# Expert results in four tables ordered by when a token's experts run; three tables are loaded and added while the last three experts run

## The reference, cut to what matters

```python
w, idx = _gate(xf, wg)                      # 4 of 32 experts for each token, with weights
fe = idx.reshape(-1)
pos = (cumsum(one_hot(fe)) * one_hot(fe)).sum(-1) - 1
dest = where(pos < cap, fe * cap + pos, E * cap)      # cap = 640 rows for each expert
xe = xp[buf_tok].reshape(E, cap, DIM)
h = silu(xe @ w1) * (xe @ w3)               # for each expert
out = (h @ w2) * buf_w
y = zeros.at[buf_tok].add(out)              # a token gets the sum of its four results
z = silu(xf @ sw1) * (xf @ sw3) @ sw2       # the shared expert
x = layernorm(xf + y + z)
```

## Time and profile before

| | us |
|---|---|
| median of three runs | 968.32 (965.99 to 975.98) |
| profiled execution | 962.11 |
| its span, first to last instruction | 960.4 |

### The profile page before, as it was taken

One profiled execution on the slowest core, in us unless ns is written; L12 is line 12 of the kernel. 1 busy time (PEld: TensorE's weight loads), 2 busy tenths in 40 slices (PEclk: granted clock), 3 DMA queues, 4 the chain that ended last, 5 costly groups with the idle time before them and its releaser, 6 DMA issues.

```text
span 960.4 us, 26130 instructions
## 1 busy us (share of the span) xinstructions
PE 817.0 (85%) x9489; PEld 594.5 (62%) x9489; DVE 673.9 (70%) x2532; ACT 650.1 (68%) x1262; POOL 681.7 (71%) x580
## 2 busy tenths in 40 slices
PE   4889999999999999999999999873377778786765
PEld 2367777777777777777777777762145555554532
DVE  6667788987987987987897897766255445545417
ACT  3678888888888798898798787864155444444405
POOL 7556565699699689689779869654656576676646
PEclk9799999999999999999999999997789898989979
DMA  5697797743453355345434433133358676566448
GB/s 159 152 297 220 241 249 202 188 121 97 97 147 98 71 140 131 73 108 133 104 90 125 116 80 98 35 91 93 74 117 175 150 168 139 144 152 140 103 157 302
DMA packets 164432, 133.88 MB, mean 139 GB/s; under 512 B 69907, under 2 KB 131654, under 8 KB 163408
## 3 DMA queue, kind: packets, MB, share of 16 engines
q1 hardware_dynamic: 155408, 116.60, 47.4%
q0 software_dynamic: 8896, 15.61, 5.7%
HBM read 31.19 MB, written 39.49 MB: 74 GB/s over the span
## 4 chain that ended last, share of the span: by engine, by line
PE 63%; issue 9%; DVE 7%; DMA 6%; ACT 6%; SPq 5%; another core or an unknown queue 3%; POOL 1%; ACTq 0%; DVEq 0%; POOLq 0%
PE PS L1328 8%; PE PS L1385 6%; PE PS L1359 4%; PE PS L1409 4%; PE PS L1392 4%; PE PS L1390 4%; PE PS L1342 3%; PE PS L1224 3%; PE PS L1411 3%; PE PS L1410 3%; PE PS L1438 3%; PE PS L1439 3%; PE PS L1183 3%; SPq L2503 2%
## 5 line engine op out<-in xcount | busy, mean ns | idle before, releaser
L2328 POOL TENSOR_TENSOR PL<-PF,PH 128x1280 f16<-128x1280 f32 x121 | 317.7, 2626 | 105.6 <-ACT PH L1674 66.6
L1943 DVE CUSTOM_DVE_ANT_0 JUNK<-PS,M 128x256 f16<-128x256 f32 (+3 forms) x512 | 225.3, 485 | 43.6 <-PE PS L1359 40.8
L1668 ACT ACTIVATE PF<-PS 128x512 f32<-128x512 f32 (+1 forms) x384 | 193.2, 520 | 77.3 <-PE PS L1392 74.3
L2371 POOL DMA_INDIRECT y_rows<-BIG,PLACE x150 | 153.0, 1020 | 85.7 <-ACT BIG L1568 48.0
L1674 ACT ACTIVATE PH<-PF 128x1280 f16<-128x1280 f32 x128 | 162.2, 1267 | 0.6
L2361 POOL DMA_INDIRECT xe_rows<-PAY,DEST x128 | 130.2, 1017 | 43.8 <-issue 27.7
L1385 PE MATMUL PS<-Q,K 128*128 128x512 f16 (+3 forms) x512 | 147.9, 299 | 6.9 <-DMA Q<-MROW 3.7
L1409 PE MATMUL PS<-VH,PH 128*128 128x65 f16 x1280 | 140.2, 195 | 11.4 <-DVE Y L1985 7.4
L1411 PE MATMUL PS<-VH,PL 128*128 128x65 f16 x1280 | 140.1, 193 | 0.1
L1410 PE MATMUL PS<-VL,PH 128*128 128x64 f16 x1280 | 140.1, 194 | 0.0
L1409 PEld LDWEIGHTS PS<-VH,PH 128*128 128x128 f16 x1280 | 119.1, 97 | 31.2 <-issue 20.1
(11 more groups left out here) (287 smaller groups left out, 2146.6 us busy)
## 6 DMA issues: line engine op xcount, KB each, us to landing
K<-KH SPq DMA_DIRECT2D x128, 128.0 KB, 2.3
Q<-QH SPq DMA_DIRECT2D x128, 128.0 KB, 2.4
xe_rows<-PAY SPq DMA_DIRECT2D x20, 520.0 KB, 4.1
Q<-xe_rows SPq DMA_DIRECT2D x30, 325.0 KB
K<-KL SPq DMA_DIRECT2D x64, 128.0 KB, 2.3
Q<-QL SPq DMA_DIRECT2D x64, 128.0 KB, 2.4
y_rows<-PAY SPq DMA_DIRECT2D x16, 512.0 KB, 4.9
K<-in_L_ffn_w_dram SPq DMA_DIRECT2D x78, 64.0 KB
```

The source lines that it names most:

```text
L1668: e.activation(PF[:, n % PBUF, c0:c0 + width], PS[:, k, 0:width], ACT.Exp).then_inc(s["c_exp"], 1)
L1943: e.tensor_tensor_reduce(JUNK[:, n_ttr % 2, 0:width], PS[:, base + ab, c0:c0 + width], M0[:, 512 - width:512], 1.0, -3e38, ALU.add, ALU.ma ...
L2328: e.tensor_tensor(PL[:, n % PBUF, :], PF[:, n % PBUF, :], PH[:, n % PBUF, :], ALU.subtract).then_inc(s["c_lp"], 1)
L2371: e.indirect_dma_start(out=y4[:, :], out_offset=bass.IndirectOffsetOnAxis(ap=PLACE[:, x_ % 8, k:k + 1], axis=0), in_=rows_of(x_)[:, k, :], ...
```

## The change

The experts now run from 29 down to 0. Word 128 of a payload becomes the token plus 4096 times a rank: the number of the token's chosen experts with a higher number, that is of those that run earlier. DVE works it out in three steps: comparisons of the four choices with each other (`ahead`), their sum (`ahead sum`), and the row (`payi`); POOL's iotas go. `y_rows` so falls into four tables with one row for each token. Since experts 0, 1 and 2 can't be of a lower rank than 3, 2 and 1, table 0 is complete when expert 3 has run (`x_` = 26), and each further expert completes one more.

SP loads table k once the rows of expert 3 - k are out, eight loads of 256 KB each. The first three tables go into buffers that are no longer used (`EARLIER`), and DVE adds them to `X1` (`share add`): table 0 for batches 0 to 6 behind the step `hidden` of the last expert, the rest behind all other steps. The fourth is added by PE: `begin` now waits for the addition of table 2 to its batch, and one matmul in place of two closes the bank. All eight openings stand ahead of the first closing matmul, as before. POOL's sums and DVE's addition L2232 go; statistics and scaling read PSUM, and the result goes to a buffer of its own.

```diff
 def expert(x_):
-    return NE - NA + x_ if x_ < NA else x_ - NA
+    return NE - 1 - x_
...
+        if x_ == NE - 2:
+            for b in range(NB - 1):
+                step("share add", 0, b)
+    step("share add", 0, NB - 1)
+    for k in (1, 2):
+        for b in range(NB):
+            step("share add", k, b)
...
+    BANK = (0, 1, 2, 5, 6, 7, 3, 4, 0)
+    def landed(k, b):
+        return (l_y4[b], 8 * k + 8) if k % 2 else (l_xa[b], 8 * k + 32)
+    def share_of(k, b):
+        return EARLIER[NB * k + b] if k < TOPK - 1 else FINAL[b]
...
         def begin(i):
             b, q0, q1 = parts[i]
...
-            w.wait_ge(s_acc, 2 * (i - 8) + 1)
+            w.wait_ge(s_share, NB * (TOPK - 2) + b + 1)
+            w.wait_ge(s_x2, i - NB + 1)
...
-        for i in range(8):
+        for i in range(NB):
             begin(i)
         for i, (b, q0, q1) in enumerate(parts):
-            w.wait_ge(l_y4[i], 16)
-            e.matmul(part, IDF[:, :], y_of(b)[:, q0:q1, 0, :], start=False, stop=False)
-            e.matmul(part, IDF[:, :], y_of(b)[:, q0:q1, 1, :], start=False, stop=True).then_inc(s_xy, 1)
+            if i >= NB:
+                begin(i)
+            w.wait_ge(*landed(TOPK - 1, b))
+            t = slice(128 * q0, 128 * q1)
+            e.matmul(PS[:, BANK[i], t], IDF[:, :], share_of(TOPK - 1, b)[:, t], start=False, stop=True).then_inc(s_xy, 1)
...
+            elif name == "ahead":
+                e.tensor_tensor(AH[:, q0:q1, :, :], chosen(b)[:, q0:q1, :].unsqueeze(3).broadcast_to(wide4),
+                                chosen(b)[:, q0:q1, :].unsqueeze(2).broadcast_to(wide4), ALU.is_lt).then_inc(s["c_dv"], 1)
+            elif name == "ahead sum":
+                e.tensor_reduce(AHS[:, q, :].rearrange("p q k -> p (q k)"),
+                                AH[:, q, :, :].rearrange("p q k e -> p (q k) e"), AX, ALU.add).then_inc(s["c_dv"], 1)
+            elif name == "payi":
+                e.scalar_tensor_tensor(out=PAY[:, q0:q1, :, 128].bitcast(I32), in0=AHS[:, q0:q1, :], scalar=float(N),
+                                       in1=TOK[:, 4 * b + q0:4 * b + q1].unsqueeze(2).broadcast_to((128, q1 - q0, 4)),
+                                       op0=ALU.mult, op1=ALU.add).then_inc(s["c_dv"], 1)
...
+            elif name == "share add":
+                k, b = a
+                w.wait_ge(*landed(k, b))
+                w.wait_ge(s_dacc, before_in_batch(len(DENSE), b))
+                w.wait_ge(s_share, NB * (k - 1) + b + 1)
+                x1b = X1[:, 4 * b:4 * b + 4, :].rearrange("p q c -> p (q c)")
+                e.tensor_tensor(x1b, x1b, share_of(k, b), ALU.add).then_inc(s_share, 1)
...
-                w.wait_ge(s_pair, i + 1)
-                e.tensor_tensor(sums_of(i, 0)[:, 0:n, :], PS[:, i % 8, 0:128 * n].rearrange("p (q c) -> p q c", c=128),
-                                PR[:, i % 3, 0:n, :], ALU.add).then_inc(s_acc, 1)
...
-                    r = e.bn_stats(st[:, q, :], sums_of(i, 0)[:, q, :])
+                    r = e.bn_stats(st[:, q, :], sum_of(i)[:, q, :])
...
+        for k in range(TOPK):
+            ended = NE - TOPK + 1 + k
...
+            for j in range(4):
+                w.wait_ge(s_ys[j], 80 * len(range(j, ended, 4)))
+            for b in range(NB):
+                w.wait_ge(*(landed(k - 2, b) if k > 1 else (None, 0)))
+                e.dma_start(share_of(k, b), y4_s[k, b]).then_inc(landed(k, b)[0], 16)
```

More of the change, by code:

```diff
@@ L500, in finish @@
         yield
+        dv("ahead")
         yield from wait(6)
@@ L510, in finish @@
             unlock(("base", b))
+        dv("ahead sum")
         yield
@@ L533, in finish @@
             for h in (0, 1):
-                marks["dest", b, h], marks["payw", b, h] = marks["dest", b], marks["payw", b]
+                for name in ("dest", "payw", "payi"):
+                    marks[name, b, h] = marks[name, b]
     def last_unit():
@@ L1017, in program @@
     s_gp = sem("s_gp")
-    l_xa, l_y4 = [sem(f"l_xa{i}") for i in range(NB)], [sem(f"l_y4{i}") for i in range(NB + 1)]
+    l_xa = [sem(f"l_xa{i}") for i in range(NB)]
+    l_y4 = [sem(f"l_y4{i}") for i in range(NB)]
     s_ys, s_out = [sem(f"s_ys{i}") for i in range(4)], [sem(f"s_out{i}") for i in range(NB + 1)]
@@ L1833, in dense_times, with before_in_batch @@
             e.tensor_tensor(DH[:, i % 2, :], PS[:, 6, :], DSIL[:, i % 2, :], ALU.mult).then_inc(s_dh, 1)
-        def before_in_batch(i):
-            return max((k + 1 for k in range(i) if DENSE[k][1] == DENSE[i][1]), default=0)
+        def before_in_batch(i, b):
+            return max((k + 1 for k in range(i) if DENSE[k][1] == b), default=0)
         def dense_add(i):
@@ L2178, in vector @@
                                 ALU.mult).then_inc(s["c_dv"], 1)
+            elif name == "ahead":
+                b, *half = a
+                q0, q1 = span(*half)
+                w.wait_ge(*(at("index float", b, *half)))
+                wide4 = (128, q1 - q0, 4, 4)
+                wide4 = (128, q1 - q0, 4, 4)
+                e.tensor_tensor(AH[:, q0:q1, :, :], chosen(b)[:, q0:q1, :].unsqueeze(3).broadcast_to(wide4),
+                                chosen(b)[:, q0:q1, :].unsqueeze(2).broadcast_to(wide4), ALU.is_lt).then_inc(s["c_dv"], 1)
+            elif name == "ahead sum":
+                b, *half = a
+                q = slice(*span(*half))
+                w.wait_ge(*at("ahead", *a))
+                e.tensor_reduce(AHS[:, q, :].rearrange("p q k -> p (q k)"),
+                                AH[:, q, :, :].rearrange("p q k e -> p (q k) e"), AX, ALU.add).then_inc(s["c_dv"], 1)
+            elif name == "payi":
+                b, *half = a
+                q0, q1 = span(*half)
+                w.wait_ge(*at("ahead sum", *a))
+                for h in half or (0, 1):
+                    w.wait_ge(*at("scat", b - 1, h))
+                w.wait_ge(*at("filled", 0))
+                w.wait_ge(s_const, 1)
+                e.scalar_tensor_tensor(out=PAY[:, q0:q1, :, 128].bitcast(I32), in0=AHS[:, q0:q1, :], scalar=float(N),
+                                       in1=TOK[:, 4 * b + q0:4 * b + q1].unsqueeze(2).broadcast_to((128, q1 - q0, 4)),
+                                       op0=ALU.mult, op1=ALU.add).then_inc(s["c_dv"], 1)
             elif name == "kept":
```

101 lines of the change are left out of this document (47 added, 54 removed).

## The result

The change makes the kernel slower: 998.86 us median (995.29 to 1009.07, four runs) against 972.15 us (965.99 to 981.99, four runs) for the kernel before; the ratio is 1.0345 (95% interval 1.0297 to 1.0393). I had forecast 965.8 us. The profiled execution took 1001.88 us, its span is 1000.1 us. Some executions of a kernel run slower than its others: the ratios leave them out, and the profiles of e2_order, e4_psum, e9_reduce and e10_sumlate, from which the argument takes the attention stage, fell on such ones (978 to 984 us).

The account below looks back on a forecast made before the run. Bound taken: the tail, 8.5 us from the last rows' landing to DVE's first step, then DVE. Tail -3.1 plus routing 0.6 gave -2.5 us on 968.3: 965.8 us, own range 961 to 971, outer range 957 to 973.

Parts of the forecast that it names:

- Placing the rows: Attention stage: three small DVE operations per batch replace POOL's iotas, mostly hidden; 0.6 us in all, bounds 0 and 5.
- the rule of the exclusive lock: SBUF ports shared by DVE and POOL: first holder blocks the other; taken to hold for DVE, not for POOL.
- The tail: From the last expert to the end: later start, shorter DVE period; span 957.3 us instead of 960.4, 3.1 us less.
- Additions: 24 on DVE behind the last multiplication, 0.62 us each, bounds 0.60 and 0.72.
- the eight openings: Opening matmuls on PE, waiting for the additions and starting at the low clock; 8.99 us, bounds 6.9 and 13.7.
- the issues: POOL's five row issues of the last expert, stretched beside DVE's additions; 1.5 us in all, 3 at most.
- the cover of table 3: Slack between its first load landing at 929.6 and PE wanting it at 937.0; 7 us.
- Rival 1: Tail: the additions hide and only the loads count; 958.8 us, chance 0.10.
- rival 4: Tail: tables wait for more than their own experts, loads start late, additions wait; about 974 us, chance 0.04.
- Rival 2: Tail: POOL's five issues block DVE's additions, 4.85 us later for all that follows; 970.7 us, chance 0.08.
- Rival 3: Tail: additions take 1.35 us each, as L1908's median beside POOL computing, instead of 0.68; 979 us, chance 0.06.
- The sign that I had named: Attention stage: the prediction is wrong if this stage moves by more than 2 us.

Follow-up runs that it names:

- e2_order: The kernel before with only the order of the experts reversed; 968.57 us, ratio 1.0013.
- e4_psum: As e3_moved, with one operand of the whole batches' comparison copied by DVE to PSUM and read there; 975.97 us, ratio 1.0056.
- e9_reduce: e3_moved plus a reduction of the same 128 x 64 numbers, SBUF to SBUF, at the comparison's first place; 966.94 us, ratio 0.9985.
- e10_sumlate: The changed kernel with the sum over the comparisons moved from ahead of the picks to behind them; 971.21 us, ratio 1.0038.
- e3_moved: The changed kernel with the whole batches' comparison moved 2 us later, behind DVE's sum of the places; 966.07 us, ratio 0.9998.
- e6_two: e3_moved plus a stand-in at the comparison's first place, the comparison itself with two SBUF operands; 1000.18 us, ratio 1.0342.
- e1_alone: The kernel before with only the comparison added, its result unused; 987.29 us, ratio 1.0207.
- e5_one: e3_moved plus a comparison with a constant, one SBUF operand, at the comparison's first place; 998.76 us, ratio 1.0287.
- e8_noadds: e3_moved without the 24 additions of tables 0 to 2, loads kept, output incomplete; 959.58 us, ratio 0.9896.

## Why the prediction was wrong

**The step that failed is "Placing the rows".** I took 0.6 us with bounds of 0 and 5; in the profiles it cost 37.6 us. The count was right (three operations, 0.2 us each: in e3_moved, where nothing holds them, 213 ns for the comparison, and a batch is 0.2 us longer). The price was wrong, because I took it from L2071, an operation at another place, and bounded it by the free time of DVE as if an operation's length did not depend on what POOL does meanwhile. The row that should have set the upper bound was in my own list: L1908 takes 687 ns or up to 1419, a two-input operation in this very stage. I used it for the additions of the tail, where POOL only issues DMAs, and not for the comparison in the attention stage, where POOL's subtractions, 121 of 2.62 us, fill 317.6 us. At 1.35 us instead of 0.2 the comparison alone would have been 8 us for seven batches, outside the bounds; that the kernel's other operations would be pushed into the subtractions is a second effect, and the fall of the clock behind PE's waiting a third, and a price for each operation shows neither.

**What takes its place**, as the runs showed: the comparison is held to the end of the subtraction into which it starts (e3_moved against e6_two, and e9_reduce for the kind of operation); this delays the end of a batch by 2 us (e1_alone); with the sum's 0.2 us more, the last pick misses the gap in front of the next subtraction by 0.08 us and is held too, and DF behind it (e10_sumlate). Held time 5.4 us, loss 6.3 us for each of six batches: 38 us. Of a batch's loss PE spends some 4.4 us waiting and 1.7 us at the lower clock; that the clock falls because of the waiting is only read from the traces: it falls in six batches of the changed kernel and of e5_one, in five of e6_two, in one of e4_psum, and in none of e1_alone and e10_sumlate, but no run here changed the clock alone.

**On the port.** I cited the rule of the exclusive lock and wrote that for POOL as the holder the trace does not agree, since L1794 started at its usual time inside a DMA issue. That was true of the issue and wrong as a conclusion about POOL. The Trainium skill, page SBUF — State Buffer, section "SBUF: two separate sides", limits the case of two SBUF inputs to "only against a GpSimd op that reads SBUF", and I left that half-sentence out; the runs agree with it for the subtraction: the comparison took 2.3 us, 2.1 of them at a standstill.

**The tail: right in sum, with its terms.** Additions 0.60 to 0.67 us apart where I took 0.62; the eight openings 9.30 us for 8.99; first statistics 23.5 us after the multiplication for 22.45; from there to the end 18.7 us for 19.3; together -2.7 us for -3.1. Granted clock 0.50 first and 1.00 at the end, as forecast. Two terms were mis-sized without effect on the sum. POOL's last issue ended 14.1 us after the multiplication for 10.4 before, so the issues cost 3.7 us and not 1.5, since the last expert but one's are stretched as well. And the cover of table 3 was 1.9 us (landed at 978.49, wanted at 980.39), not 7: besides the issues, the last rows landed 4.0 us after the end of their issue instead of 1.1 us; at that time the DMA engines were full with table 2 (share 1.04). e8_noadds shows 4.2 us there too, without any addition.

**The rivals.** Rival 1 (the additions hide) and rival 4 (loads too late) did not come true; table 2 made DVE wait for 1.5 us in all. Rival 2 (issues hold up the additions) did not: they keep their 0.60 us beside issues. Rival 3 was nearest, operations of DVE that take longer beside POOL's arithmetic, but at the wrong place and in the wrong manner: I read L1908 as running at half its speed, and in the trace of before the five of its seven that are longest start inside a subtraction and end 0.55 us behind it, so they were held:

```profile
191.17 2.63 POOL L2328 TENSOR_TENSOR PL<-PF,PH 128x1280 f16<-128x1280 f32 x1 [0.33 <-issue]
192.94 1.40 DVE L1908 TENSOR_TENSOR BIG<-X,BIG 128x512 f16<-128x512 f32 x1
```

The sign that I had named, that the attention stage moves by more than 2 us, is what showed it; but kernels with nothing held moved it by 1 to 8 us too, so 2 us was too fine a sign.

## What to carry to other kernels

Before an operation of DVE is put somewhere, look at what POOL computes at that time; beside a POOL operation on two operands from SBUF, a DVE operation of a kind that is held (here those with two operands from SBUF, and the comparison with a constant) has its time set by the slot and not by its length. Take the price from operations of the same kind in the same stage, with their spread and not their least value: a group with 687/1348/1419 ns was a sign that some of its kind are held. In a schedule in which operations stand clear of such a window by 0.1 to 0.3 us, 0.2 us more work ahead of them can cost 4 us a batch, so ask of every added operation what it pushes, too.

## What the runs showed that I had not expected

A comparison with a constant (one operand in SBUF, f32 to bf16, 128 x 64) is held by POOL's subtraction as long as one with two operands: 2298 against 2337 ns, where a reduction of the same numbers takes 209. What decides is which of the two starts first: in all six batches of e10_sumlate a pick that began 0.05 us ahead of the subtraction kept its 0.28 us and the subtraction took 2.72 us instead of 2.62; in the changed kernel a pick that began 0.08 us behind it took 2.7 us. Beside POOL's DMA issues it is the other way round: the additions keep their 0.60 us whether an issue runs or not, and the issues grow from 0.97 to 1.50 us.
